# Order of a block sum and a tile's filter on TensorE in a graph network's edge loop

## The reference

```python
# layer 0
agg = segment_sum(edge_weight[:, None] * x[src], dst)
x   = layernorm(x + relu((x + agg) @ W1 + b1) @ W2 + b2)
# layer 1: here the roles of the two ends are exchanged
h1  = x @ lin1_w.T
c   = 0.5 * (cos(edge_weight * pi / 10) + 1)
f   = softplus(edge_attr @ nn_w1.T + nn_b1) - log 2
W   = (softplus(f @ nn_w2.T + nn_b2) - log 2) * c[:, None]
agg = segment_sum(W * h1[dst], src)
x   = layernorm(x + (h1 + agg) @ lin2_w.T + lin2_b)
```

## Time and profile before

| | |
|---|---|
| median of 2 runs | 8774.0 us (8772.1 to 8775.9) |
| the profiled execution, its own time | 8796.3 us |
| its span | 8794.7 us |
| busy over the span: GpSimd, TensorE, VectorE, ScalarE | 71%, 67%, 67%, 39% |
| TensorE's weight loads | 54% |
| mean granted TensorE clock | 0.738 of full |

### The profile page before, as it was taken

How to read it: one execution, slowest core, us unless ns; L and a number is a source line. 1 busy time by engine, 2 the same in 40 slices (tenths; PEclk the granted TensorE clock), 3 DMA queues, 4 the chain that set the end, 5 groups by cost and what they waited for, 6 DMA issues and landing times. The chain is left out here.

```text
span 8794.7 us, 201979 instructions
## 1 busy us (share of the span) xinstructions
PE 5927.9 (67%) x35386; PEld 4731.0 (54%) x35658; DVE 5851.1 (67%) x17865; ACT 3465.1 (39%) x6782; POOL 6213.8 (71%) x6560
## 2 busy tenths in 40 slices
PE   5676676667676676666655556666767666666787
PEld 3444444444444444444444445666666666666676
DVE  6666666666666666665655556777777777777776
ACT  3434344443444444444544443334444343443302
POOL 6777777777777777775377777777777777777710
PEclk7766676666776767667755557888888888888897
DMA  5444454444444445444444446666666666666676
GB/s 165 154 152 153 150 155 151 154 151 152 154 153 153 153 153 153 153 153 148 143 133 134 135 131 191 212 213 213 213 215 213 212 215 211 215 215 211 215 238 203
DMA packets 805506, 1537.47 MB, mean 175 GB/s; under 512 B 193406, under 2 KB 207156, under 8 KB 804963
## 3 DMA queue, kind: packets, MB, share of 16 engines
q1 hardware_dynamic: 595415, 1097.64, 38.8%
q0 software_dynamic: 209712, 436.16, 16.9%
q10 hardware_dynamic: 348, 3.33, 0.1%
HBM read 971.97 MB, written 564.58 MB: 175 GB/s over the span
## 5 line engine op out<-in xcount | busy, mean ns | idle before, releaser
L1353 POOL DMA_INDIRECT sorted_messages<-rows,sidx x3224 | 3115.5, 966 | 1153.4 <-issue 946.9
L516 POOL DMA_INDIRECT xg<-x_rows,gidx x3224 | 3050.4, 946 | 1032.8 <-issue 858.9
L584 PE MATMUL bank<-attr,nn 128*128 128x512 f32 x1612 | 1484.7, 1075 | 191.0 <-DMA attr<-attr_cols 181.6
L573 PE MATMUL bank<-onehot,xg 128*128 128x42 f32 x6448 | 945.1, 303 | 845.5 <-DMA xg<-x_rows,gidx 838.1
L1281 PE MATMUL bank<-hot,block_rows 128*128 128x128 f32 x8256 | 1390.0, 344 | 30.0 <-DVE hot L1435 29.9
L1281 PEld LDWEIGHTS bank<-hot,block_rows 128*128 128x128 f32 x8256 | 1342.8, 258 | 55.7 <-issue 17.8
L573 PEld LDWEIGHTS bank<-onehot,xg 128*128 128x128 f32 x6448 | 877.1, 212 | 882.0 <-DMA xg<-x_rows,gidx 874.4
L1251 PE MATMUL bank<-w_nn2T,e_hid 128*128 128x128 f32 x6448 | 1041.9, 314 | 293.1 <-DMA e_hid<-hidden 285.2
L1251 PEld LDWEIGHTS bank<-w_nn2T,e_hid 128*128 128x128 f32 x6448 | 1008.2, 226 | 250.3 <-DMA e_hid<-hidden 217.2
L465 ACT ACTIVATE soft<-bank 128x512 f32<-128x512 f32 x808 | 475.3, 588 | 1332.8 <-PE bank L584 1332.5
L1262 PE MATMUL bank<-h1w,ohT 128*128 128x128 bf16 x3224 | 337.9, 268 | 982.1 <-DVE ohT L1382 982.1
(11 more groups left out here) (220 smaller groups left out, 8235.4 us busy)
## 6 DMA issues: line engine op xcount, KB each, us to landing
block_rows<-sorted_messages SPq DMA_DIRECT2D x346, 792.0 KB
hidden<-hid SPq DMA_DIRECT2D x404, 512.0 KB
e_hid<-hidden SPq DMA_DIRECT2D x403, 512.0 KB
sorted_messages<-zero SPq DMA_DIRECT2D x403, 264.0 KB
dstb<-dst SPq DMA_DIRECT2D x403, 256.0 KB
attr<-attr_cols SPq DMA_DIRECT2D x403, 204.0 KB
xg<-x_rows,gidx POOLq DMA_INDIRECT x3224
sorted_messages<-rows,sidx POOLq DMA_INDIRECT x3224
```

The costliest lines, as they stand in the source:

```text
L516: pool.indirect_dma_start(xg[b][s][:, :], None, x_rows, bass.IndirectOffsetOnAxis(ap=gidx[b][s // HALF][:, s % HALF:s % HALF + 1], axis=0) ...
L573: nc.tensor.matmul(bank[0][:, 0:WIN], xg[b][s][:, :], onehot[:, s, :], start=(s == 0), stop=(s == SUB - 1)).then_inc(summed[b], 1)
L584: nc.tensor.matmul(bank[2 + h][:, :], nn1[:, :], attr[:, h, :], start=True, stop=True).then_inc(z1_set, 1)
L1353: pool.indirect_dma_start(table, bass.IndirectOffsetOnAxis(ap=sidx[b][h][:, s:s + 1], axis=0), rows[b][h][:, s, :], None).then_inc(landed[ ...
```

## The change

In the second loop TensorE does the sums of a turn ahead of the tile that they run beside, where it did the tile first. The other engines' programs, the first loop and the third stay as they were.

```diff
             with pe.Fori(0, pairs) as c:
                 for k in range(2):
+                    sum_turn(first_slot(c, k), k)
                     windows_of(c * 2 + (alone + k))
-                    sum_turn(first_slot(c, k), k)
             with pe.Fori(0, tail_rounds(pe)) as r:
```

## The result

The changed kernel takes 10066.7 us (median of 2 runs, 10064.5 to 10069.0) where the kernel before took 8774.0: 1.1475 times as long, with an interval of 1.1455 to 1.1495. 10240 was forecast, with a range of 9930 to 10600.

What follows compares the result with a forecast made beforehand. GpSimd's queue was taken to bound the loop at 10.17 us a tile. A 15.12 us ring over 298 tiles adds 1475 us, less 8, to the profiled 8796.3: 10263, less 22, predicted as 10240 us; range 9930 to 10600.

Steps and rivals of the forecast that it cites:

- GpSimd bounds the loop before, and VectorE has half a microsecond to spare: Loop with sums, before: GpSimd's scatters set 10.17 us a tile; VectorE needs 9.63 us.
- a ring: Loop with sums: one-hots of t-1, sums, filter, softplus, messages, adds and one-hots of t, each waiting for the one before.
- The ring's length: Steps laid end to end per tile: 12.25 us at the high clock, 15.12 us with the sums at the low level.
- the sums at the low clock: TensorE's three blocks take 5.43 us, ending 3.84 us behind the third one-hot in place of 0.97.
- The other terms: Filter's first half 1.50 us, activations 1.92, `filt` to `filt` 2.09, `filt` to first add 3.30, adds and one-hots 2.47.
- the block of 4.54 us: Earlier turn with the clock low for a part only, three blocks in 4.54 us: would give 14.23 us a tile, 9976 us.
- The clock falls in each tile's idle time: TensorE idles 6.5 us a tile, so its clock drops to 1.2 GHz and the sums start at half rate.
- rival 1: TensorE's clock stays high in the loop with sums: 612 us more, 9386 us; chance 0.06.
- SyncE's loads, VectorE's waits for sums, the loop's end: Loads cost 0; VectorE's 57.0 us of waits go without gain; GpSimd ends at most 4.4 us behind, giving back 8 us.
- Rival 2: The low clock lasts through the filter in the loop with sums: 16.15 us a tile, 10548 us; chance 0.10.
- The profiled execution's 22 us: Whole kernel before: the median lies 22 us below the profiled 8796.3 us, so 10263 became 10240 us.

Runs made afterwards that it cites:

- The memset run: Kernel before with a scrap memset on GpSimd ahead of the third scatter in each half of each layer 1 tile: 8832.3 us beside 8771.2.
- the run with the sums between: Kernel before with the turn's sums placed after the tile's two filter halves and ahead of its node rows: 8797.6 us (6 runs), 1.0031 times.
- the filler run: Changed kernel, column numbers in SBUF, plus 32 unread TensorE products behind each tile of the loop: 9471.2 us, 591 below its control.
- the two runs with short bursts: Changed kernel with only the first of three blocks summed ahead of the tile, 9470.7 us; and with one product of four per block, 9571.3 us.

## Why the prediction was right, step by step

- **GpSimd bounds the loop before, and VectorE has half a microsecond to spare.** Right. The memset run shows the first; the second is in VectorE's waits for landings, 148.6 us in 290 tiles. The 28 us of the run with the sums between don't show it, since longer scatters account for 26 of them.
- **The waits moved ahead of the filter close a ring.** Right: the filter behind them carries nearly all (10066.7 against 8797.6 us with only the node rows behind), and ScalarE's time counts only in the changed order.
- **The ring's length.** 15.12 us forecast, 14.51 measured. The term that was mis-sized is the sums at the low clock, 3.84 us, measured 3.11 on average. 0.23 of that is a slip of mine: I counted to the end of the last product, while the filter's first weight load starts before it, so that even the longest was 3.61 (first weight load at 7018.52, sums until 7018.94). 0.50 is the clock, which came back sooner in most tiles: of 297, only 74 had the 3.6 us of the late return, and the others lay between 2.5 and 3.3. I took the nearest row, that of the late return, for all, where the earlier trace rows had the block of 4.54 us. The other terms were each within 0.13 us and cancel out (+0.26 and -0.15). 0.61 x 298 is 182 us, and the forecast was 173 too high; the tile before, taken as 10.17 where it is usually 10.14, made it some 10 us too low.
- **The clock falls in each tile's idle time.** Right, and the filler run priced it: 591 us. The Trainium skill's rule (page "TensorE: Matmul & The Clock Gate", section "HAM oscillation — how this bites in real kernels"), told there for waits on a DMA: a loop whose steps hold a long wait starts each step cold. The changed kernel's rows agree, with waits on VectorE: the sums' term is 2.54 to 3.61 us in every tile, and 1.19 at full clock. The ring costs more than the clock: 9471 us are left at full clock, and rival 1's 9386 was its sum with 12.25 for 12.51.
- **SyncE's loads, VectorE's waits for sums, the loop's end.** Loads of hidden rows and blocks are in no wait of the changed loop; the 57.0 us are gone without a gain; 7 us came back at the end for the 8 forecast. GpSimd ended 5.1 us behind VectorE, not 4.4 at most. The loop's start 10 us sooner is not the change's: the profiled execution of the kernel before was late by then.
- **Rival 2, the filter at the low clock too.** Not in the changed kernel, but it is what the two runs with short bursts fell into.
- **The profiled execution's 22 us.** I took them off, which puts the gain per tile on the median of the kernel before. That was right, though the rows didn't say where the 22 us lay. The changed kernel's profiled execution was within 3 us of its median. Some 10 us of the slow execution were in the 10.17 us of a tile, where they stayed.

No order tried beats the kernel before: its pace is GpSimd's, and no order of TensorE's work made GpSimd faster.

## What to carry to other kernels

Here a wait delayed all that stood behind it in the engine's queue: the filter, whose inputs were there, started 5.9 us after the first one-hot's start. Before moving a step with a wait ahead of others, name who consumes their results and follow that chain: if it comes back to what the wait is for, the whole chain can become the period, however idle each engine is; it does when it is longer than what sets the pace now, as 14.5 us against 10.2 here. Put work whose input has long been there ahead of work whose input comes last. And price a step at the clock that its new place has, the steps behind it too.

## What the runs showed that I had not expected

- The time from the start of work to the clock's return isn't one number: 3.1 us and 6.2 us in neighbouring tiles of the changed kernel, so that a tile's length took values from 13.81 to 15.56. With a ring of 13.65 us it was the late one each time, so shortening one step by 1.3 us gave 0.86.
- Adding 32 useless products a tile made the changed kernel 591 us faster.
- A GpSimd instruction between two scatters cost 0.08 us, not its 0.22, and a semaphore increment there nothing.
- A scatter that starts 0.1 us into VectorE's `ohT` takes 1.20 us instead of 0.96, and with the sums between filter and node rows, where they meet in nearly every second tile, longer scatters account for 26 of the 28 us.
- The one-hot compare takes 0.68 us in the median whether its row of column numbers is read from PSUM or from SBUF; from PSUM none took over 0.69, from SBUF some took up to 0.77.
